# A four-layer graph network on one core: marks by source beside a node product, 11 scattered columns in the sheaf stage, sums by source in pieces of 250

## The reference

```python
x = _layernorm(x + L0(x))   # two graph attention layers, softmax over the edges of a destination
x = _layernorm(x + L1(x))   # messages of edges, silu, summed by source, node product
x = _layernorm(x + L2(x))   # the sheaf layer, below
x = _layernorm(x + L3(x))   # edge matrices times neighbours, summed by source
```

```python
xs, xd = x[src], x[dst]
F_s = householder(reflection(xs, xd)); F_d = householder(reflection(xd, xs))
L_sd = -jnp.einsum('eki,ekj->eij', F_s, F_d)
msg_s = coef[:, None] * jnp.einsum('eij,ej->ei', L_sd, xd)
msg_d = coef[:, None] * jnp.einsum('eji,ej->ei', L_sd, xs)
out = x - zeros.at[src].add(msg_s) - zeros.at[dst].add(msg_d)
```

## Time and profile before

| what | us |
|---|---|
| median of 3 runs | 25102.21 (25093.5 to 25139.49) |
| the profiled execution | 25105.15 |
| its span, first to last instruction | 25103.4 |
| sheaf stage, in the span | 13795 to 20255 |
| three sums by source start at | 12944.6, 20265.9, 24718.9 |
| segments by source, scatters start at | 4354.3 |
| mean granted clock of TensorE | 0.723 |

### The profile page before, as it was taken

The page is one execution under the profiler, slowest core; times in us unless marked ns, Lnnn a source line. Parts: engine busy times, 40 slices in busy tenths (PEclk is TensorE's granted clock), DMA queues, the critical chain, the costliest instruction groups (busy, mean ns, idle before and its releaser), DMA issues. The chain is left out here.

```text
span 25103.4 us, 351859 instructions
## 1 busy us (share of the span) xinstructions
PE 15996.3 (64%) x99053; PEld 11741.1 (47%) x99056; DVE 16286.5 (65%) x41450; ACT 3853.7 (15%) x8407; POOL 18136.2 (72%) x17443
## 2 busy tenths in 40 slices
PE   4211110266666647888853888888888838999993
PEld 3211110155555535666633454455545516777772
DVE  7679976177777726777761666666666645666664
ACT  0000000122222211111100111111111101222220
POOL 5777777677777737777753777777777767888884
PEclk7555555555555557888875889888888867888886
DMA  3211111011111101111120111111111120101012
GB/s 103 82 35 43 44 37 30 14 31 31 31 31 31 31 10 25 25 25 25 25 79 7 20 19 20 19 19 20 20 19 19 20 72 24 26 25 26 25 26 74
DMA packets 1007292, 810.94 MB, mean 32 GB/s; under 512 B 579829, under 2 KB 897503, under 8 KB 1003105
## 3 DMA queue, kind: packets, MB, share of 16 engines
q0 software_dynamic: 557728, 189.18, 6.0%
q1 hardware_dynamic: 348648, 290.30, 4.3%
q10 hardware_dynamic: 100800, 330.28, 3.4%
HBM read 414.80 MB, written 393.60 MB: 32 GB/s over the span
## 5 line engine op out<-in xcount | busy, mean ns | idle before, releaser
L1513 POOL DMA_INDIRECT msgs<-msg_msg,msg_pos x4875 | 5730.9, 1176 | 1550.8 <-issue 1485.0
L1748 POOL DMA_INDIRECT sheaf_got<-table,sheaf_idx x3125 | 3180.1, 1018 | 952.8 <-issue 952.8
L977 POOL DMA_INDIRECT gat_got<-table,gat_idx x3125 | 2963.5, 948 | 953.9 <-issue 952.1
L1410 PE MATMUL msg_dps<-msg_dhotq,msg_dleft 128*128 x16500 | 3517.4, 377 | 0.0
L1410 PE MATMUL sheaf_dps<-sheaf_dhotq,sheaf_dleft 128*128 x18000 | 3341.7, 343 | 0.9 <-DVE sheaf_dhotq L1393 0.9
L988 POOL DMA_INDIRECT ring<-table,src_all x2325 | 2217.2, 954 | 733.2 <-issue 707.9
L1410 PEld LDWEIGHTS msg_dps<-msg_dhotq,msg_dleft 128*128 x16500 | 1840.1, 116 | 1397.5 <-issue 650.2
L1319 PE MATMUL place_look_ps<-place_nexts,place_hot_at 98*128 98x128 f32 x5000 | 1624.0, 465 | 1330.4 <-DVE place_same L1224 929.5
L1410 PEld LDWEIGHTS sheaf_dps<-sheaf_dhotq,sheaf_dleft 128*128 x18000 | 1820.5, 102 | 1310.0 <-issue 260.0
L1622 ACT COPY msg_flip<-msg_fps 128x384 f32<-128x384 f32 (+1 forms) x3000 | 1357.7, 493 | 5281.3 <-PE msg_fps L1580 5272.3
L1756 POOL DMA_INDIRECT msgs<-sheaf_msg,sheaf_pos x1625 | 1787.9, 1100 | 519.7 <-issue 519.7
(11 more groups left out here) (463 smaller groups left out, 29550.8 us busy)
## 6 DMA issues: line engine op xcount, KB each, us to landing
msg_ex<-ex SPq DMA_DIRECT2D x250, 400.0 KB
gat_sums<-gat_acc ACTq DMA_DIRECT2D x125, 675.0 KB
msgs<-msg_msg,msg_pos POOLq DMA_INDIRECT x4875
tail_m<-msgs SPq DMA_DIRECT2D x75, 800.0 KB
src_sums<-tail_acc ACTq DMA_DIRECT2D x75, 800.0 KB
gat_sums<-gat_acc ACTq DMA_DIRECT2D x125, 425.0 KB
ring<-table,src_all POOLq DMA_INDIRECT x3125
ex<-zeros ACTq DMA_DIRECT2D x25, 2000.0 KB
```

What stands on the lines that cost most here:

```text
L977: pool.indirect_dma_start(got[b][:, j, :], None, table, bass.IndirectOffsetOnAxis(idx[b][:, j:j + 1], 0)).then_inc(gathered[b], 16)
L1410: last = pe.matmul(self.acc[:, n, 0:self.BQ], left, hot_q, start=False, stop=False, skip_group_check=True)
L1513: pool.indirect_dma_start(msgs, bass.IndirectOffsetOnAxis(pos[b][:, j:j + 1], 0), msg[b][:, j, :], None).then_inc(scattered[b], 16)
L1748: pool.indirect_dma_start(got[b][:, j, :], None, table3, bass.IndirectOffsetOnAxis(idx[b][:, j:j + 1], 0)).then_inc(gathered[b], 16)
```

## The change

Three edits go together.

1. `find_segments("s")` is cut in three. `find_places` stays where it was and works out starts, ends and places. `put_marks`, the 128 scatters, becomes a part of the block of `hidden2`, on POOL. `find_segments_by_source`, the load of the marks and what follows, is a block of its own behind the first layer's normalization. The tile of the marks lives until then.
2. `CP_2` goes from 13 to 11: in the sheaf stage 11 columns of a chunk are scattered and 14 are direct. Their columns are spread over the eight groups as 1, 2, 2, 2, 1, 2, 2, 2 (before 1, 2, 1, 2, 1, 2, 1, 2).
3. `sum_by_source` runs in `RUNS` = 10 pieces of `LONG` = 250 places (25 of 100 before), with buffers of that size. The tile `direct` is no longer held for the whole kernel; each of the three stages allocates its own.

```diff
-CP_1, CP_2, CP_3 = 19, 13, 20
+CP_1, CP_2, CP_3 = 19, 11, 20
...
-    CT = C_S // NCT
+    RUNS = NCT // 5 * 2
+    LONG = C_S // RUNS
...
-        direct = sb("direct", [NP, NK, D])
+        settled = {}
...
-        def find_segments(o):
+        def find_places(mark):
...
-                    dve.tensor_copy(g["take"][:, :], tmp[:, :]).then_inc(marked, 1)
-                    dve.wait_ge(got, 16)
-                    ch.add(dve.tensor_scalar(keep[o][:, :], mk[:, :, 1], 0.0, None, ALU.is_equal))
+                    ch.link(dve.tensor_copy(g["take"][:, :], tmp[:, :]))
...
+        def put_marks(pool, mark, put_done):
+
+            for k in range(NK):
+                pool.indirect_dma_start(marks["s"], bass.IndirectOffsetOnAxis(order["s"]["put"][:, k:k + 1], 0),
+                                        mark[:, k, :], None, bounds_check=P * C_S - 1, oob_is_err=False
+                                        ).then_inc(put_done, 16)
+            pool.wait_ge(put_done, 16 * NK)
+
+        def find_segments_by_source():
...
+                    ch.add(dve.memset(row2[:, 0:1], 0.0))
+                    dve.wait_ge(got, 16)
                     dve.tensor_reduce(top[:, :], mk[:, :, :].rearrange("p c w -> p w c"), AX_X, ALU.max).then_inc(topped, 1)
+                    ch.add(dve.tensor_scalar(keep[o][:, :], mk[:, :, 1], 0.0, None, ALU.is_equal))
...
                 @block.sync
                 def _(sp):
-                    sp.wait_ge(put_done, 16 * NK)
                     sp.dma_start(mk[:, :, :], edges(marks[o])).then_inc(got, 16)
...
+                if beside:
+                    @block.gpsimd
+                    def _(pool):
+                        beside(pool, was_put)
...
-                m = [sb(f"{name}_m{b}", [P, CT, D], F32, ctx) for b in range(2)]
-                acc = [sb(f"{name}_acc{b}", [P, CT, D], F32, ctx) for b in range(2)]
+                m = [sb(f"{name}_m{b}", [P, LONG, D], F32, ctx) for b in range(2)]
+                acc = [sb(f"{name}_acc{b}", [P, LONG, D], F32, ctx) for b in range(2)]
...
-                        sp.dma_start(m[b][:, :, :], msg_v[:, bass.ds(i * CT, CT), :]).then_inc(loaded[b], 16)
-                    run_turns(sp, NCT, body)
+                        sp.dma_start(m[b][:, :, :], msg_v[:, bass.ds(i * LONG, LONG), :]).then_inc(loaded[b], 16)
+                    run_turns(sp, RUNS, body)
...
-            find_segments("s")
+            mark_s = sb("mark_s", [NP, NK, 2], F32, ctx)
+            find_places(mark_s)
...
-                             middle=(ident[0:C2, 0:C2], C2, selu_of(b2c[:, 0:1], b2c[:, 1:2], b2c[:, 2:3])))
+                             middle=(ident[0:C2, 0:C2], C2, selu_of(b2c[:, 0:1], b2c[:, 1:2], b2c[:, 2:3])),
+                             beside=lambda pool, put_done: put_marks(pool, mark_s, put_done))
...
                 layer_norm("norm0", y0, x_cur)
+            find_segments_by_source()
...
+            settled["sums"] = sb("direct2", [NP, NK, D], F32, ctx)
             settle_direct("settle2")
```

More of the change, by code:

```diff
@@ L491, in _ @@
                                             ).then_inc(looked, 16)
-        def find_segments(o):
-            g, cols = order[o], cols_of[o]
+        def find_places(mark):
+            g = order["s"]
             with ExitStack() as ctx:
[L498 to L510, removed]
+                incl, end = sb("incl_s", [NP, NK], F32, ctx), sb("end_s", [NP, NK], F32, ctx)
+                tmp, zero = sb("tmp_s", [NP, NK], F32, ctx), sb("zero_s", [NP, NK], F32, ctx)
+                v = sb("v_s", [P, 1], F32, ctx)
+                ps = ctx.enter_context(nc.psum_tensor("ps_s", [P, 512], F32))
+                steps, totals, offs = (sem(f"places_{n}") for n in ("steps", "totals", "offs"))
                 block = ctx.enter_context(nc.Block())
@@ L522, in _ @@
                     ch.link(dve.tensor_tensor(g["start"][:, :], end[:, :], cnt[:, :], ALU.subtract))
-                    if o == "s":
-                        ch.add(dve.tensor_tensor(free_place[:, :, :], free_place[:, :, :],
-                                                 g["start"][:, :].unsqueeze(1).to_broadcast([NP, LANES, NK]), ALU.add))
+                    ch.add(dve.tensor_tensor(free_place[:, :, :], free_place[:, :, :],
+                                             g["start"][:, :].unsqueeze(1).to_broadcast([NP, LANES, NK]), ALU.add))
                     ch.add(dve.tensor_scalar(mark[:, :, 0], g["start"][:, :], 1.0, None, ALU.add))
@@ L566, in _, with node_product @@
                     pe.transpose(ps[:, 256:258], row2[:, 0:P], ident[0:2, 0:2]).then_inc(backed, 1)
[L568 to L574, removed]
                 @block.sync
                 def _(sp):
-                    sp.wait_ge(put_done, 16 * NK)
                     sp.dma_start(mk[:, :, :], edges(marks[o])).then_inc(got, 16)
-        def node_product(name, widths, fill, weights, cols, use, middle=None, taken=None, put=None, store=None):
+        def node_product(name, widths, fill, weights, cols, use, middle=None, taken=None, put=None, store=None, beside=None):
             groups = NK // GK
@@ L1442, in _ @@
                         dve.wait_ge(turned, 4 * n + 4)
-                        dve.tensor_copy(direct[:, 32 * n:32 * n + 32, :].rearrange("p k f -> p (k f)"), ps[n][0:NP, :])
+                        dve.tensor_copy(settled["sums"][:, 32 * n:32 * n + 32, :].rearrange("p k f -> p (k f)"), ps[n][0:NP, :])
         def both_sums(dve, ch, seg):
@@ L1448, in both_sums @@
                                       order["s"]["has"][:, :].unsqueeze(2).to_broadcast([NP, NK, D]), ALU.mult))
-            ch.link(dve.tensor_tensor(seg[:, :, :], seg[:, :, :], direct[:, :, :], ALU.add))
+            ch.link(dve.tensor_tensor(seg[:, :, :], seg[:, :, :], settled["sums"][:, :, :], ALU.add))
         def messages(name, attr, fills, outer_of, weights, finish, cp, exponential=False):
@@ L2155, in gnn_kernel @@
             renew_semaphores()
+            settled["sums"] = sb("direct1", [NP, NK, D], F32, ctx)
             settle_direct("settle1")
@@ L2168, in fill_sums @@
                                               order["s"]["has"][:, group].unsqueeze(2).to_broadcast([NP, GK, D]), ALU.mult))
-                    return dve.tensor_tensor(stage[:, :, :], stage[:, :, :], direct[:, group, :], ALU.add)
+                    return dve.tensor_tensor(stage[:, :, :], stage[:, :, :], settled["sums"][:, group, :], ALU.add)
                 node_product("agg1", [D], fill_sums, [lin[:, :]], D, into(agg, norm_lin), taken=("s", src_sums, seg3))
@@ L2273, in gnn_kernel @@
             renew_semaphores()
+            settled["sums"] = sb("direct3", [NP, NK, D], F32, ctx)
             settle_direct("settle3")
```

41 lines of the change are left out of this document (28 added, 13 removed).

## The result

The changed kernel takes **24676.71 us** (median of 3 runs, 24674.34 to 24708.92), where it took 25102.21 before: a ratio of 0.9831 (95% interval 0.9808 to 0.9853), 425 us less. The prediction was 24600, 504 us less. The profiled execution after took 24708.92 us (span 24707.2).

What follows compares the result with a forecast made beforehand. POOL was taken to bound the sheaf stage, PE some 8 us a chunk behind. Columns 284, marks 165 and pieces 55 sum to 504 us off 25105: 24601, on the median's footing 24598, rounded to 24600 us; range 24510 to 24780.

Steps and rivals of the forecast that it cites:

- two rivals that did not happen: Sheaf stage: PE becomes its limit, 24775 us, chance 0.20; or added one-hots hold POOL, 24755 us, chance 0.08.
- What bounds the sheaf stage: Sheaf stage: POOL's gathers and scatters with their issue time fill all 6440 us; PE next, some 8 us a chunk behind.
- The removed scatters: Sheaf stage: two scatters fewer a chunk save POOL the bare price, 2 x 1.27 = 2.54 us a chunk.
- The added stretch, 0.21 us a chunk: Sheaf stage: direct-column products grow by 0.85 us a chunk and slow POOL's gathers beside them, costing POOL 0.21.
- The one-hots cost POOL nothing: Sheaf stage: two more one-hots of 0.63 us a chunk on DVE leave POOL's gathers at 0.94 us.
- The rival that charged POOL their whole length: Sheaf stage: two added one-hots cost POOL 1.26 us a chunk, 347 us off in all, 24755 us; chance 0.08.
- the sentence of the Trainium skill that was weighed there: One-hots in the sheaf stage: `tensor_scalar` can hold the port through which POOL writes descriptors, `tensor_tensor` not; saving would be halved.
- PE takes over: Sheaf stage: PE at clock 0.88 and 98% busy needs 50.6 us a chunk; 326 us off, 24775 us; chance 0.20.
- The end of the stage: Sheaf stage's end: nothing covers PE, so its added columns in the last two chunks cost 7 us.
- The marks: The 128 scatters move beside a product of 190 us and are hidden with 25 us to spare: 165 us off.
- The pieces: Sums by source in pieces of 250: 27.6 us off each in the first and third, nothing in the second; 55 us.

Runs made afterwards that it cites:

- the probe: Changed kernel plus a block of eleven stretches, each with 12 POOL gathers beside one repeated VectorE instruction; one profiled execution, gathers 0.94 to 1.95 us.
- 5, 5, 4: Changed kernel with the sheaf stage's three products for 14 direct columns each cut into 5, 5 and 4 columns: 24507.6 us, ratio 0.9754.
- 3, 3, 3, 3: Changed kernel with 13 scattered columns again and the sheaf stage's products for 12 direct columns cut into 3, 3, 3 and 3: 24756.0 us, ratio 0.9866.
- 7, 7: Changed kernel with the sheaf stage's three products for 14 direct columns each cut into halves of 7: 24700.1 us, ratio 0.9831.
- 5, 5, 2: Changed kernel with 13 scattered columns again and the sheaf stage's products for 12 direct columns cut into 5, 5 and 2: 24887.9 us, ratio 0.9913.

## Why the prediction was right, and where it was off

The time lay in the range and on the right side; the sum was 77 us too large, all of it and more from one term, of which the pieces, worth more than forecast, hid a part. The range covered this by luck: its slow end, 24780, stood for two rivals that did not happen, and the miss that did happen was not among its bounds.

- **What bounds the sheaf stage**: right. POOL's idle time is all "issue" after the change as before it, and with PE as the next, 3.2 us behind instead of the 2 forecast.
- **The removed scatters**, 2 x 1.27 = 2.54 us a chunk: right. Profiles give 2.53 and, between the run with 13 columns and the repeat of the changed kernel, 2321.3 - 2004.3 = 317 us, 2.54.
- **The added stretch, 0.21 us a chunk: the step that failed.** The prediction took "the rate of stretch beside it, 0.42 us in 1.66", and let it grow with the 0.85 us that the products grew. A gather isn't slowed at a rate. Each waits to the end of a product, so all three gathers pay the whole growth of one, 3 x (1.94 - 1.67) = 0.81, and the first waits longer as well. In the profile it is 1.06 a chunk; by the trace some 0.9 of it lies with the gathers beside these products, the rest with gathers beside shorter instructions. Net 1.47 instead of 2.33. The numbers to see it were in the earlier trace rows: 1.36 and 0.30 to issue are the 1.67 of a product.
- **The one-hots cost POOL nothing**: right for the kernel, 0.94 beside them, but not because they leave POOL alone: in the probe they hold gathers, which costs some 0.06 us a gather, and in the kernel every second one-hot is some 0.18 longer. The rival that charged POOL their whole length, 1.26 us a chunk, falls, although its 24755 missed by hardly more than the forecast (78 and 77 us). Of the sentence of the Trainium skill that was weighed there (SBUF — State Buffer, Who interferes with whom), the half on `tensor_scalar` agrees with the probe, though not at the price of a length, and the half on `tensor_tensor` fails. The rule of that section that the experiments quote was not weighed.
- **PE takes over** (24775): did not happen; PE still waits in nearly every chunk, and POOL never does. The stage that this rival took as its example, the third message stage, was filled by POOL as well, as the version with all products cut showed.
- **The end of the stage**, 7 us lost: the stage's 175 is POOL's 183 less 8, so about right.
- **The marks**, 165: right, 171 when undone, and hidden with 27 us to spare (25 forecast).
- **The pieces**, 55: undersized; 70 by the traces, 84 when undone. First and third gained 31 and 32 instead of 27.6: pieces 11.5 us apart instead of 11.85, and a fill of 7.2 us instead of 8.85. The second, put at nothing, gained 6, which is 47 ns x 128 of its gathers: the few long ones beside the shorter scans are gone.

## What to carry to other kernels

Where POOL's indirect DMAs set the pace, look at what VectorE runs beside them and compare where each DMA ends with where those instructions end: a constant distance is a wait for an end, not a slowdown, and its price follows the length of each instruction, not the sum. Then choose that length. A cut is worth making only if some number of the pieces fits just over the DMA's own period (here 1.24 us: 5, 5, 4 or 3, 3, 3, 3 columns gained, 7, 7 and 5, 5, 2 did not), and moving one operand to PSUM, where a bank is free, takes the hold away entirely in the probe; in the kernel it was not tried.

## What the runs showed of the hardware

- Products of VectorE with both operands in SBUF held POOL's indirect DMAs to their end: 1.72 to 1.78 us instead of 0.95 beside products 2.06 us apart; with one operand in PSUM 0.94 to 0.96.
- A copy from f32 to f32 in SBUF, one operand only, held them as well (1.95 us beside copies 1.13 us apart); a reduction of the same tile did not (0.94 to 0.96). What makes the difference between these two wasn't tried.
- One-hots (tensor_scalar, int16 to bf16) held them too, at hardly any price: in the probe a gather to two one-hots of 0.66 us, 1.00 to 1.04 each.
- An engine that is busy for 98% of a stage need not be its bound: the third message stage, at 489 of 500 us for PE, gave 116 us when only products beside POOL were cut. POOL, with its issue time, had filled 499 of the 500.
